# Attention of a macaron block: k, q and their low parts taken sooner, z's columns interleaved in PSUM

## The reference, cut to what matters

```python
def attn(x, W_Q, W_K, W_V, W_O):              # x: (8, 512, 128), 16 heads of 64
    q = einsum('ahe,bce->bach', W_Q, x)
    k = einsum('ahe,bce->bach', W_K, x)
    v = einsum('ahe,bce->bach', W_V, x)
    scores = einsum('bach,baCh->bacC', k, q)  # rows by k, columns by q
    masked = where(tril, scores, -1e10)       # causal
    attn = softmax(masked / 8, axis=-1)
    z = einsum('bacC,baCh->bach', attn, v)
    return einsum('aeh,bach->bce', W_O, z)
x = x + attn(layernorm(x), ...)
```

## Time and profile before

| | us |
|---|---|
| median of 3 runs | 951.3 (951.26 to 952.12) |
| the profiled execution's own time | 942.84 |
| its span (first to last instruction) | 940.7 |
| PE busy | 859.9 (91%) |
| DVE busy | 812.2 (86%) |
| ACT busy | 674.7 (72%) |
| POOL busy | 279.9 (30%) |

### The profile page before, as it was taken

One profiled execution on the slowest core, in us unless ns is written; L12 is line 12 of the kernel. 1 busy time (PEld: TensorE's weight loads), 2 busy tenths in 40 slices (PEclk: granted clock), 3 DMA queues, 4 the chain that ended last, 5 costly groups with the idle time before them and its releaser, 6 DMA issues.

```text
span 940.7 us, 24331 instructions
## 1 busy us (share of the span) xinstructions
PE 859.9 (91%) x7378; PEld 737.2 (78%) x7378; DVE 812.2 (86%) x3083; ACT 674.7 (72%) x1977; POOL 279.9 (30%) x328
## 2 busy tenths in 40 slices
PE   7999999978999998998998998999899888999994
PEld 6889998866777777776777776777687776999994
DVE  7878888789899899899999999989989996786666
ACT  3787667577777867785877786777686775787881
POOL 5777103241111021312321312310200102567551
PEclk9999999999999999999999999999999999999998
DMA  9677556177788688777687778676766785557657
GB/s 248 217 221 245 183 156 199 46 210 175 230 227 215 206 239 215 221 209 206 187 242 182 233 204 225 190 235 199 214 195 209 185 231 159 168 159 212 218 158 225
DMA packets 141296, 190.40 MB, mean 202 GB/s; under 512 B 35328, under 2 KB 108832, under 8 KB 141168
## 3 DMA queue, kind: packets, MB, share of 16 engines
q1 hardware_dynamic: 128256, 168.56, 61.1%
q0 software_dynamic: 8352, 18.17, 7.8%
q10 hardware_dynamic: 4560, 2.12, 0.8%
HBM read 114.04 MB, written 74.74 MB: 201 GB/s over the span
## 4 chain that ended last, share of the span: by engine, by line
PE 36%; DVE 25%; issue 5%; DMA 4%; SPq 2%; ACT 0%; POOL 0%; POOLq 0%; DVEq 0%; ACTq 0%
PE psum L2552 8%; PE psum L2502 7%; DVE arena L1975 6%; PE psum L2387 5%; DVE arena L1960 4%; PE psum L2338 3%; PE psum L2340 3%; PE psum L2339 3%; DVE arena L1990 3%; DVE q_lo L1947 2%; PE psum L2585 2%; PE psum L2541 2%; DVE k_lo L1951 1%; DMA turned_dram<-arena 1%; DVE bn L1243 1%
## 5 line engine op out<-in xcount | busy, mean ns | idle before, releaser
L1130 ACT ACTIVATE arena<-arena,neg_max 128x512 f32<-128x512 f32 (+3 forms) x512 | 281.5, 553 | 145.0 <-DVE neg_max L1960 142.7
L1960 DVE CUSTOM_DVE_ANT_0 arena<-psum,causal 128x512 f32<-128x512 f32 (+3 forms) x512 | 217.1, 480 | 29.0 <-PE psum L2502 28.5
L1074 ACT ACTIVATE arena<-psum,b_t 128x256 f32<-128x256 f32 (+1 forms) x336 | 120.8, 442 | 40.6 <-PE psum L2340 31.4
L876 POOL DMA_INDIRECT arena<-y_tiles,y_at x64 | 61.0, 953 | 277.6 <-PE psum L2502 194.3
L2387 PE MATMUL psum<-w_sb,arena 128*128 x1136 | 141.5, 276 | 0.2 <-ACT arena L1074 0.2
L2387 PEld LDWEIGHTS psum<-w_sb,arena 128*128 128x128 f32 x1136 | 134.9, 193 | 0.4 <-issue 0.4
L857 POOL DMA_INDIRECT x_slots<-xr,slot x64 | 61.9, 968 | 237.9 <-PE psum L2502 190.1
L2502 PE MATMUL psum<-q_hi,k_lo 64*128 64x512 f32 (+3 forms) x512 | 87.0, 332 | 42.0 <-DVE q_lo L1947 41.8
L1975 DVE STREAM_TRANSPOSE arena<-arena 128x768 f32<-128x768 f32 x126 | 115.7, 960 | 4.7 <-DMA turned_dram<-arena 2.8
L2502 PEld LDWEIGHTS psum<-q_hi,k_lo 64*128 64x128 f32 x512 | 49.0, 185 | 70.6 <-DVE q_lo L1947 65.0
L1130 ACT ACTIVATION_READ_ACCUMULATOR arena<-arena,neg_max 128x1 f32 x512 | 97.4, 190 | 0.0
(11 more groups left out here) (361 smaller groups left out, 1989.9 us busy)
## 6 DMA issues: line engine op xcount, KB each, us to landing
turned_dram<-arena SPq DMA_DIRECT2D x252, 192.0 KB
y_all<-turned_dram SPq DMA_DIRECT2D x63, 768.0 KB, 5.2
arena<-inv_dram SPq DMA_DIRECT2D x128, 128.0 KB
w_raw<-in_L_ffn_W_dram SPq DMA_DIRECT2D x60, 256.0 KB
xg<-x_slots SPq DMA_DIRECT2D x43, 144.0 KB
arena<-in_L_ffn_W_dram SPq DMA_DIRECT2D x24, 256.0 KB
arena<-y_rows SPq DMA_DIRECT2D x16, 256.0 KB, 4.8
y_tiles<-y_all SPq DMA_DIRECT2D x27, 128.0 KB, 1.9
```

Of the source, the lines that this page charges most:

```text
L1074: ins = act.activation(h_t[side(f, n)][:, k, 0:rows], H_BANKS[side(f, n)][k // 2][:, k % 2 * rows:(k % 2 + 1) * rows], ACT.Relu, bias=b1_t ...
L1130: ins = act.activation(prob_tile(i, h, t), prob_tile(i, h, t), ACT.Exp, scale=-1.0, bias=neg_max[i % 2][:, h, t:t + 1], accum_out=row_sum[ ...
L1960: ins = dve.tensor_tensor_reduce(out=prob_tile(i, h, t), in0=score_tile(t, h), in1=causal[:, SEQ - (t + 1) * P:SEQ], scale=-1.0, scalar=-2 ...
```

## The change

`max_ready` counts four uses a step instead of three: tile 3 of the first head, tile 3 of the second, tile 2, tiles 1 and 0. ACT begins the exponential of the first head after the first of them. ACT takes k and q of the next step behind the exponentials of tile 2 instead of behind those of tile 1. DVE takes their low parts behind `divide_by_sums`, ahead of `turn_long` and of the other work. PE writes z with row q of tile t at column q*4+t; `divide_by_sums` reads PSUM and `inv_bc` side by side and writes `z_sb`, whose layout stays, in steps of 128 elements (512 bytes) from tile to tile.

```diff
-        S_USES, EXPS, PT_USES, PT_ACT, V_PAIRS = 3, 4, 2, 2, 4
+        S_USES, MAXES, EXPS, PT_USES, PT_ACT, V_PAIRS = 3, 4, 4, 2, 2, 4
...
+        Z_TILES = RING_C.rearrange("p (q t) -> p t q", t=QT)
...
             def exps(i, t):
-                act.wait_ge(max_ready, S_USES * i + min(QT - t, S_USES))
                 for h in range(2):
+                    act.wait_ge(max_ready, MAXES * i + (1 + h if t == QT - 1 else min(QT + 1 - t, MAXES)))
                     ins = act.activation(prob_tile(i, h, t), prob_tile(i, h, t), ACT.Exp, scale=-1.0,
...
                     exps(i, 3)
                     exps(i, 2)
-                    exps(i, 1)
                     if i + 1 < STEPS:
                         take_k(i + 1)
                         take_q(i + 1)
+                    exps(i, 1)
                     if i > 0:
                         transposed(i - 1)
                     exps(i, 0)
...
-            def maxima(i, use, tiles):
+            def maxima(i, use, tiles, heads=range(2)):
...
-                    for h in range(2):
+                    for h in heads:
...
-                dve.tensor_tensor(z_sb.rearrange("p (t q) -> p t q", t=QT), RING_C.rearrange("p (t q) -> p t q", t=QT),
-                                  inv_bc[i % 2].rearrange("p q t -> p t q"), ALU.mult).then_inc(z_ready, 1)
+                dve.tensor_tensor(z_sb.rearrange("p (t q) -> p q t", t=QT), RING_C.rearrange("p (q t) -> p q t", t=QT),
+                                  inv_bc[i % 2], ALU.mult).then_inc(z_ready, 1)
...
-                    maxima(i, 0, [3])
+                    maxima(i, 0, [3], [0])
+                    maxima(i, 0, [3], [1])
                     if i > 0:
                         invert(i - 1)
                     maxima(i, 1, [2])
                     maxima(i, 2, [1, 0])
                     if i > 1:
                         divide_by_sums(i - 2)
+                    if i + 1 < STEPS:
+                        split_k(i + 1)
+                        split_q(i + 1)
                     if i < STEPS - 1:
                         turn_long(i)
                     if i == STEPS - 2:
                         finish(work)
                     go_on(work, 4)
-                    if i + 1 < STEPS:
-                        split_k(i + 1)
-                        split_q(i + 1)
...
-                    return pe.matmul(RING_C[h * DH:(h + 1) * DH, tiles.start * P:tiles.stop * P], value(k, h), squares, start=start, stop=stop)
+                    return pe.matmul(Z_TILES[h * DH:(h + 1) * DH, tiles.start:tiles.stop, :], value(k, h), squares, start=start, stop=stop)
...
-                    pe.wait_ge(max_ready, S_USES * i + 2)
+                    pe.wait_ge(max_ready, MAXES * i + 3)
...
-                    pe.wait_ge(max_ready, S_USES * (i + 1))
+                    pe.wait_ge(max_ready, MAXES * (i + 1))
...
-                pe.wait_ge(max_ready, S_USES * STEPS)
+                pe.wait_ge(max_ready, MAXES * STEPS)
```

## The result

The changed kernel takes 963.9 us in the median of its runs (961.8 to 970.5), the kernel before in the same set 951.3 (951.0 to 952.1): a ratio of 1.0143, interval 1.0092 to 1.0194. Forecast were 943, so the sign was wrong and the size by 21 us. On another chip it was 1.0189 (1.0156 to 1.0221).

What follows compares the result with a forecast made beforehand. PE and DVE were taken to bound the kernel by waiting for each other, PE mostly for q_lo. 9.5 us from seven batches plus 2 from batch 0, less 3 for the late squares, gave 951.3 - 8.5 = 943 us, range 937 to 982.

Steps and rivals of the forecast that it cites:

- the late squares: Squares stored to DRAM and loaded for attend, stored later behind the later transposes: 3 us given back, bounds 0 and 14.
- B: Attend's matmuls on PE: strided PSUM writes slow them, up to 2.3 us a step, 1045 us in all; chance 0.20.
- C: DVE's division: the strided store of z_sb costs more than the strided read did, 1.9 us; 976 in all; chance 0.07.
- the walk: Step-by-step sum of PE and DVE over a batch: 73.4 us, 73.8 with 0.35 added, against 75.1.
- Part 1: ACT's exponentials begin one maximum earlier, 0.73 us after the first maximum's start, not 1.34; alone it gains nothing.
- Part 2: ACT takes k and q ahead of tile 1's exponentials: PE has q_lo 1.8 us sooner; plain-step floor 8.65 us.
- Part 3: DVE's low parts ahead of the transposes, which end 9.15 us after the first score, not 7.34; DVE idles up to 0.7.
- Part 4: z interleaved: DVE's division takes 0.88 us, a saving of 0.2 a step; PE's strided writes cost nothing.
- the four rules: Formulas for each next step's first score and first maximum, from PE's surplus, DVE's busy time and DVE's lag.
- The gain: PE's earlier q_lo saves 1.35 us a batch, 9.5 in seven batches; with 2 in batch 0, 11.5 together.
- A: The late squares become the bound: their way takes 12.2 us, not 11.1, and attend waits; 954 in all; chance 0.15.
- D: ACT reaches k no sooner because tile 2's maxima hold its exponentials; only DVE's order changes; 949 to 953; chance 0.08.

Runs made afterwards that it cites:

- additions later: Changed kernel with GpSimd's two additions of a batch's results one step later (JOIN_STEP 6, not 5): 1.0086 against the kernel before, +8.0 us.
- transposes first: Changed kernel with the block transposes ahead of the low parts, both still ahead of the other work: 0.9967, in a repeat 0.9977, against the kernel before.
- sets 2 and 3: Run groups on chips where the kernel before took 945.2 and 944.6 us: changed kernel +16.3 us in the first, with GpSimd's additions one step later +8.0 in the second.
- The exception in set 4: In step 4 of batches 0 and 7 the low parts go behind the other work; changed kernel with this and GpSimd's additions later: 1.0043 against the kernel before.
- set 1: First follow-up runs, on a chip with the kernel before at 998.5 us; z's interleaved layout alone, put into the kernel before, took 0.9969 of its time.
- the run without the three: Changed kernel, GpSimd's additions later, low parts behind other work in step 4 of batches 0 and 7, no wait for late squares: 1.0043 against before, +4.5 us.

## Why the prediction was wrong

Two steps failed. The sum took a gain of 1.35 us a batch from PE's earlier q_lo, and an undisturbed batch gained nothing (75.1 us). And behind "low parts ahead of the transposes" it priced, besides the late squares, only 0.15 us a batch for the scores of step 5 that wait for DVE's work of step 4. That wait is 0.7 us in each of six batches, 1.65 where GpSimd's addition holds DVE up, and in batches 0 and 7 PE waits for other pieces of that work. The measured 963.9 lies within the stated 937 to 982 only because the range was drawn wide for rivals B and C, which didn't occur.

Steps in us, cut at the first score matmul:

```
step                         0     1     2     3     4     5     6     7    sum
before, batch 4            8.73  9.25 10.39  9.39  9.92  8.88  9.31  9.24  75.11
the walk                   8.73  8.65  8.87 10.20  9.28  9.75  9.31  8.65  73.44
the walk, put right        8.75  8.75  9.96  9.47  9.64  9.01  9.31  8.75  73.64
changed, batch 4           8.78  8.82  9.86  9.74  9.77 10.80  9.63  8.77  76.15
changed, batch 6           8.77  8.75  9.86  9.75  9.79  9.80  9.62  8.75  75.09
additions later, batch 4   8.77  8.74  9.88  9.73  9.78  9.82  9.64  8.75  75.11
transposes first, batch 4  8.77  8.77  9.72  9.89  9.61  9.34  9.64  8.77  74.51
```

**Part 1** was run only together with ACT's half of part 2; the two bring nothing, as forecast.

**Part 2** was right in its times (q_lo, k_hi to 0.02). The floor of a plain step is 8.75 and not 8.65: ACT's second copy ends at S+8.61, as added up, but PE goes on 0.14 later. I had 0.03 for that. By the walk that is 0.12 us a batch. The copy of v, 0.2 in the sum, is seen in step 6: 9.62 and not 9.31.

**Part 3** was right in the end of the transposes and wrong in what hangs on it. The walk priced the order by DVE's sum and by q_hi, and for the end of the other work it had only the 0.15. What the other work meets there I did not ask, and GpSimd stands nowhere in the prediction. Its additions begin 1.05 us behind the first score of step 5, since PE's scores release them (542.94, S being 541.89). DVE had fallen 1.4 us further behind PE (its first maximum of step 4 comes 2.91 us behind PE's first score, before 1.49), and the work had gone back in DVE's list by the low parts, 1.1 us. The xr operations, before over 1.25 us ahead of step 5's first score, thus slid under the addition. Four batches at 0.98 are 3.9 us; between sets 2 and 3 the medians say 8.3, and what the other 4 are isn't shown. The page "SBUF — State Buffer" of the Trainium skill, section "Who interferes with whom", says why: VectorE and GpSimd share one pair of ports, and a `tensor_scalar` from memory to memory in its two-port mode and a GpSimd instruction lock each other out for a whole instruction, the first to start winning. By that rule the one that comes second is blocked to the other's end. No row shows the mode or the ports. In its times the trace agrees (1.31 us in place of 0.34, ending 0.09 after the addition), and so does the rule's other half: xn_lo and the maxima, with one input from PSUM, ran beside the second addition in their usual 0.68.

The same part put the other work behind the low parts in step 4 of batches 0 and 7, where PE reads its products at once. The earlier trace rows showed batch 4 alone, and the walk was carried over to all eight. PE waits 2.4 us for xr in batch 7 (before 1.3) and 2.9 for the normalised rows in batch 0 (before 2.3). For two of DVE's routing pieces it waits in batch 7 as well: 1.1 us for hits in step 4 (before none) and 2.4 for count_bf in step 6 (before 0.8). The exception in set 4 gives 1.2 us of that back by the traces, 4 by the times, as far as two chips can be compared.

**Part 4** failed in half. That PE's strided writes cost nothing was right, against the rule of the Trainium skill (PSUM — Partial Sum Buffer, Specifications (TRN2)) which gave rival B: 517 ns before, 517 and 514 with a step of 16 bytes. Attend's stretch stayed at 2.31 us too. The saving at the division was mis-sized: 0.2 expected, -0.002 measured in its duration and 0.065 in the start of the next instruction. By duration, writing in steps of 512 bytes costs the 0.4 us that reading in steps of 16 bytes did. Walked again with 0.065, the four rules give 0.4 us a batch more, of the 1.3 by which batch 6 misses 73.8.

**The late squares** were given 3 us, 0 to 14. Measured: 6.9 with the collision there, and nothing to be measured once it and step 4 are gone. The mechanism held (SP waits 131.3 us for stores, not 15.8), but most of what it cost came only together with the other stalls. How a stall of PE makes a load late, with step lengths that repeat otherwise, I can't show.

**The gain** of 9.5 in batches 1 to 7 is what failed most. Steps 7, 1 and 2 gave back 0.5 us each, as the wait for q_lo had cost, and steps 3, 5 and 6 took 0.35, 0.9 and 0.3 again. Before, PE's wait for q_lo let DVE catch up, so that it was early in the next heavy step. Removing it moved the wait: PE now waits 17.7 us for tile 2's maxima, and not 2.9.

The walk also took its T from the wrong cut. The earlier trace rows are cut at PE's first score, but the rules use T from one first maximum to the next. The other work of step 1 thus stood in step 2. Cut at the first maxima, DVE is busy 8.47, 10.04, 9.39, 9.37, 8.98, 7.45, 8.26 and 8.38 us in steps 0 to 7 of batch 4, as here in step 1:

```profile
491.39:501.66 10.27, 9.52 (x91) 7.67 (x87) 10.04 (x35) 6.88 (x21) 2.66 (x3) 1.00 0.89 233
```

With these T, 0.065 saved and a floor of 8.75 the four rules give the third row of the table. Its sum hardly moves, but steps 2 and 4 come out as measured in batch 6, within 0.15. With the 0.35 it is 74.0 against 75.1. Of the 1.1 left, 0.53 is the wait for xn_lo (0.68, in the sum with 0.15) and 0.1 the copy of v. The rest is open. Batch 0 did give in its first step what was forecast for it (6.47 us, before 8.17), and lost it again in steps 2 and 4, to the late squares and the normalised rows.

Of the rivals, A had the right sign and its place in part (954 forecast) but not the main cause; B and C fell with set 1; D fell, as q_lo did come sooner.

**Settled and open.** The loss is in DVE's order (1.0189 with it, 0.9983 without); it goes by 8 of 16.3 us with GpSimd's additions moved and by 4 more with step 4, each as compared between chips. 4.5 us remain. They lie at the two ends: with the additions later and the exception in step 4, batches 1 to 6 take 451.3 us together (before 451.7), batch 0 75.6 (before 73.46) and the seven steps of batch 7 68.6 (before 67.1). In batch 7 the waits for hits and count_bf are still there, 3.5 us together where before had 0.8 and 0.8 for q_lo. In batch 0 the clock is mixed in: one and the same kernel, the one before with the low parts behind the transposes, has that batch at 75.6 us with 10.2 us at half clock in set 1, and at 72.5 with none in set 3. So what the order costs there, and how much of the 4.5 us is clock, is not shown. Over all of attention PE was at half for 13.7 us in the run without the three, for 3.4 in the kernel before and for 6.8 and 10.2 in the changed one's two traces; but also for 10.2 in the changed kernel with the transposes first and the exception, which is faster than before.

## What to carry to other kernels

Before moving work on one engine, list every instruction of the moved block and all that slide with it, and lay beside them what the other engines run at that time, GpSimd above all; then ask which other engine reads each product, batch by batch and not only in the typical one. A wait that shows in forty places may be the slack in which two engines with equal work meet: if DVE's sum per batch is as large as PE's, removing PE's wait moves it. When you walk two engines step by step, cut each one's work where its own list begins. Moving a stride from an input to the output saved 0.065 of its 0.4 us here: without a row for the new form, take no saving.

## What the runs showed of the hardware

- A four-byte matmul that writes PSUM in steps of 16 bytes takes what it took side by side (514 to 517 ns in the mean for 384 columns, 2.31 us for all of attend's matmuls of a step).
- A VectorE multiplication of 128x512 with a step of 512 bytes in its output takes 1085 ns, as with a step of 16 bytes in one input (1083); the next instruction starts 0.93 us after it and not 0.99. Subtractions of that shape, side by side in all three operands, take 671 to 685.
- A VectorE `tensor_scalar` of 128x128 stretches from 0.34 to 1.31 us when a GpSimd addition (1.26 us) starts 0.04 us ahead of it.
- After a wait of 1.66 us within the scores of step 5 of batch 3, TensorE was at 1.2 GHz for 3.4 us in set 2's run of the changed kernel, so that attend took 4.0 us (459.15 to 463.15) and not 2.31. Stretches of that run, from the wait on (the eighth column is the clock):

```profile
457.00:458.30 1.30, 0.00 (x0) 0.02 (x1) 1.30 (x3) 0.00 (x0) 1.22 (x2) 1.00 1.03 275
458.30:459.10 0.80, 0.79 (x12) 0.78 (x12) 0.80 (x3) 0.29 (x1) 0.65 (x2) 1.00 0.99 271
459.10:461.00 1.90, 1.90 (x17) 1.28 (x16) 1.90 (x10) 1.79 (x6) 1.59 (x2) 0.63 0.76 164
461.00:463.20 2.20, 2.20 (x15) 1.24 (x11) 0.52 (x6) 0.75 (x4) 0.23 (x1) 0.55 0.09 34
```

The same wait in batch 4 of that run left the clock at 1.00. So such a stall can be followed by a loss of 1.7 us more, but not each time. That the stall causes the fall of the clock is likely, not shown.
